# Attention's unit on TensorE in another order: 64-row products side by side, logits and places in a score bank

## Chip, cores and metric

One core of a Trainium2 chip. The metric is the device time of one execution in microseconds (us), as the median of several runs. Engines are called as the profile calls them: PE (TensorE's matmuls), PEld (its weight loads), DVE (VectorE), ACT (ScalarE), POOL (GpSimd), SP (SyncE).

## What is computed

Two residual layers over x of 32 sequences x 64 tokens x 512 channels. The first mixes each sequence with a chosen 64x64 matrix and applies a gated feed-forward block. The second is what the change touches: attention over a paged cache with a window of 256 keys, then a top-2 mixture over 8 experts.

```python
q, k, v = x @ Wq.T, x @ Wk.T, x @ Wv.T        # 8 query heads, 4 key heads of 64; rms norm and rotation of q and k
k_all, v_all = cache rows by block_tables, new k and v written in
scores = einsum('bghtd,bgsd->bghts', q, k_all) * SCALE      # masked to the last 256 positions
p = softmax(scores)
o = einsum('bghts,bgsd->bghtd', p, v_all) @ Wo.T
logits = clip(o @ gate_w.T, -50, 50)                        # 8 experts
top_w, top_idx = top_k(logits, 2)
rw = softmax(top_w)
out = x + o @ W.T + what the two chosen experts add, weighed by rw
```

## The kernel before

The program is written by hand for five engines. Each engine has a list of instructions that it runs in order, and semaphores tie the lists together: `wait_ge(s, n)` holds an engine's whole list until the counter s has reached n. There are three stages: layer 0 with the projections to q, k and v (to about 430 us), attention with routing (to about 770 us), and the experts. The change is in the second stage alone.

**Units.** Attention runs over `UNITS` = 64 units. Unit n takes the sequence q = n // 2 and one pair `gp` = n % 2 of the key heads. Four units (two sequences, 128 tokens) are a *pair* p = n // 4, and `at` = n % 4 is the unit's place in the pair. The loop over n on PE (L1017) is software-pipelined: its round n issues

- `score(n + 2)` (L924): six products of 320 columns, `q` by `kT`, over 64 rows (one head's 64 channels) each; the two heads lie in rows 0 to 63 and 64 to 127 and write banks 0 and 1;
- `turn_p(2n)` and `turn_p(2n + 1)` (L939): six transposes of the probabilities, over 128 rows;
- `turn_k(n + 3)` (L906): three transposes of the gathered keys. A sequence has 320 keys in three chunks of 128, 128 and 64 rows (`KCH`), so the third transpose, the *tail*, is over 64 rows;
- `values(n - 1)` (L947): the probabilities times the values, again in chunks of 128, 128 and 64 rows; each float32 product is two instructions in the trace, so that it shows six;
- at `at` = 0 `turn_q` (L917) for the next pair; at `at` = 2 `places(p - 2)` (L975), `logits(p - 1)` (L960) and `project_o(p - 1)` (L968), all over 128 rows.

**Where the keys and values come from.** POOL gathers each sequence's rows by indirect DMAs into a ring of `KVB` = 4 buffers `kv_t`: two from the cache (L541), one of new rows for the last chunk (L549), one that writes the routing list of an earlier pair from the tenth sequence on (L2084), and two that lay new rows over the cache's (L558), each of which waits until the cache's rows have landed. The gather of sequence q waits for `o_ps`, that is until the last product of `values` for sequence q - 4 has run; the transposes of its keys wait for `kv_gathered`:

```python
pool.wait_ge(o_ps, q - KVB + 1)                                  # L2091
pe.wait_ge(kv_gathered[q % KVB], (q // KVB + 1) * GATHERS)       # L910, in turn_k at gp == 0
```

So what `values` reads in the round with `at` = 2 of a pair (sequence 2p) is overwritten with sequence 2p + 4, whose keys `turn_k` takes in the round with `at` = 1 of the next pair.

**The other engines.** Per unit, ACT rounds the keys (`kT_hi`, L1197), takes exponentials (L1221) and copies the turned probabilities (`pT_copy`, L1224) and the result (`oT_copy`, L1233). DVE masks the scores (`masked`, L1780), scales the probabilities (`normalize`, L1789) and makes the low part of the keys (`kT_copy`, L1762), which the next `score` waits for. Its routing steps are `weigh`, `place_entry`, `read_logits`, `rank` and `choose` (L1804 to L1848). Logits, places and totals stand in bank 5, which also takes the turned keys; so `turn_k` at `at` = 3 waits for `lg_read`.

Of the kernel before, what the change touches and what calls it, by code (L numbers as in the profile page):

```python
# [83 lines left out]
def bass_adaln_ffn_kernel(nc, x, kv_lens, subjects, tables, cond_w, gate_t, up_t, down_t, gate_s, up_s, down_s,  # L84
# [20 lines left out]
    with ExitStack() as ctx:  # L105
# [508 lines left out]
        O_BANKS = (4, 7)  # L614

        def k_bank(n):

            return bk(2) if n == 1 else bk(5)
# [11 lines left out]
        with nc.Block() as block:  # L630
# [149 lines left out]
            def _(pe):  # L780
# [124 lines left out]

                def turn_k(n):  # L906

                    q, gp = n // 2, n % 2
                    if gp == 0:
                        pe.wait_ge(kv_gathered[q % KVB], (q // KVB + 1) * GATHERS)  # L910
                    if n >= 2:
                        pe.wait_ge(kT_ready, n)
                    for c, rows in enumerate(KCH):
                        mm = pe.transpose(k_bank(n)[:, c * P:c * P + rows], kv_t[q % KVB][0:rows, c, gp * P:(gp + 1) * P], ident[0:rows, 0:rows])  # L914
                    mm.then_inc(kT_ps, 1)
# [8 lines left out]
                def score(n):  # L924

                    p, b, gp = n // 4, n // 2 % 2, n % 2
                    if b == 0:
                        pe.wait_ge(qT_ready, p * 2 + gp + 1)
                    pe.wait_ge(kT_ready, n + 1)
                    if n >= 1:  # L930
                        pe.wait_ge(sm_ready, 2 * n)
                    for i, (q, k) in enumerate(((qT_hi, kT_hi), (qT_hi, kT_lo), (qT_lo, kT_hi))):
                        for g in range(2):
                            rows = slice(g * HD, (g + 1) * HD)
                            mm = pe.matmul(bk(g)[:, 0:KEYS], q[rows, gp, b, :, :].rearrange("p h t -> p (h t)"), k[rows, n % KRING, :],  # L935
                                           start=(i == 0), stop=(i == 2))
                    mm.then_inc(score_ps, 1)
# [22 lines left out]
                def logits(p):  # L960

                    pe.wait_ge(oT_ready, 2 * p + 2)
                    rows = oT if p < PAIRS - 1 else oT_last
                    for k in range(KT):
                        mm = pe.matmul(bk(5)[:, 0:E], rows[:, k, :, :].rearrange("p b t -> p (b t)"), wr[:, k, :], start=(k == 0), stop=(k == KT - 1))  # L965
                    mm.then_inc(lg_ps, 1)
# [8 lines left out]
                def places(p):  # L975

                    pe.wait_ge(sel_ready, p + 1)
                    pe.matmul(bk(5)[:, 2 * E:4 * E], tri[:, :], ab[:, :, :].rearrange("p a e -> p (a e)"), start=True, stop=False)
                    mm = pe.matmul(bk(5)[:, 2 * E:4 * E], ones_sq[:, :], counts[:, :, :].rearrange("p a e -> p (a e)"),
                                   start=False, stop=True)  # L980
                    if p == PAIRS - 1:
                        for n, part in enumerate((ab, counts)):
                            mm = pe.matmul(bk(5)[:, 4 * E:6 * E], ones_sq[:, :], part[:, :, :].rearrange("p a e -> p (a e)"),
                                           start=(n == 0), stop=(n == 1))
                    mm.then_inc(pos_ps, 1)
# [18 lines left out]
                fold(0)  # L1004
                fold(1)
                turn_k(0)
                turn_k(1)
                score(0)
# [4 lines left out]
                pe.wait_ge(counts_zero, 1)  # L1013
                pe.wait_ge(fold_ready, WR_DONE)
                turn_k(2)

                for n in range(UNITS):  # L1017
                    p, at = n // 4, n % 4
                    if n + 2 < UNITS:
                        score(n + 2)  # L1020
                    turn_p(2 * n)
                    turn_p(2 * n + 1)
                    if n + 3 < UNITS:
                        if at == 3 and p >= 1:
                            pe.wait_ge(lg_read, p)
                        turn_k(n + 3)
                    if n >= 1:
                        values(n - 1)
                    if at == 0 and p + 1 < PAIRS:
# [3 lines left out]
                    if at == 2 and p >= 1:  # L1033
                        pe.wait_ge(kT_ready, min(n + 4, UNITS))
                        if p >= 2:
                            places(p - 2)
                        logits(p - 1)
                        if p + 1 < PAIRS:
                            pe.wait_ge(qT_ready, 2 * p + 4)
                            project_o(p - 1)  # L1040

                final = PAIRS - 1
                values(UNITS - 1)
                places(final - 1)
                logits(final)
# [257 lines left out]
            def _(dve):  # L1303
# [500 lines left out]
                def read_logits(p):  # L1804
                    dve.wait_ge(lg_ps, p + 1)
                    dve.tensor_scalar(lg[:, :], bk(5)[:, 0:E], 50.0, -50.0, ALU.min, ALU.max).then_inc(lg_read, 1)

# [30 lines left out]

                def place_entry(p):
# [4 lines left out]
                    step(dve.tensor_tensor(chosen[:, :, :], bk(5)[:, 2 * E:4 * E].rearrange("p (a e) -> p a e", e=E), row_0[:, :, :], ALU.add),  # L1844
                         dve.tensor_tensor(counts[:, :, :], counts[:, :, :].bitcast(F32), ab[:, :, :].bitcast(F32), ALU.add))
                    step(dve.tensor_tensor(chosen[:, :, :], chosen[:, :, :], ab[:, :, :].bitcast(F32), ALU.mult))
                    step(dve.tensor_reduce(entry_row[:, p, :], chosen[:, :, :], AX, ALU.add))
# [39 lines left out]
                for n in range(UNITS):  # L1887
                    p, at = n // 4, n % 4
                    if at == 3 and p >= 1:
                        if p >= 2:  # L1890
                            place_entry(p - 2)
                        read_logits(p - 1)
                        rank(p - 1)
# [25 lines left out]
                dve.memset(seven[:, :], 0.0)  # L1919
                weigh(final - 1)  # L1920
                place_entry(final - 1)
                read_logits(final)
                rank(final)
                choose(final)
                weigh(final)
                place_entry(final)

# [7 lines left out]

                tstep(dve.tensor_scalar(total_i[:, :, :], bk(5)[:, 4 * E:6 * E].rearrange("p (a e) -> p a e", e=E), float(P - 1), None, ALU.add))
                tstep(dve.tensor_scalar(total_i[:, :, :], total_i[:, :, :], 7, None, ALU.arith_shift_right))
# [260 lines left out]
```

## Time and profile before

| | us |
|---|---|
| median of 3 runs | 949.13 |
| lowest, highest | 947.29, 950.86 |
| profiled execution, from its first to its last instruction | 947.2 |
| PE busy | 879.3 (93%) |
| PEld, DVE busy | 629.4, 658.1 |
| ACT, POOL busy | 385.0, 421.0 |

The page gives no time of the profiled execution other than its span; the lowest run is 0.1 us longer than it. A row of a timeline gives the start of a group of instructions in us from the span's start, how long the group lasted, its engine, line, operation and names, its shape as rows*columns, and in brackets how long the engine was idle before and what ended that. Ends of matmuls are modelled, so that on PE the distance from start to start tells more than the lengths.

### The profile page before, as it was taken

The page shows a single profiled execution, that of the slowest core. Times are in us where ns is not written, and L with a number is a line of the kernel's source. Part 1 is how long each engine was busy: PE and PEld are TensorE (multiplying, and loading weights), DVE is VectorE, ACT ScalarE, POOL GpSimd, SP SyncE. Part 2 cuts the span into 40 slices and gives each one's busy share as a digit, 9 for nine tenths or more (in the row PEclk, how much of TensorE's full clock was granted, in tenths as well). Part 3 has the DMA queues.
Part 4 walks back from the last instruction along what each step waited for, and adds up shares of the span by engine and source line. Part 5 has one row for each costly group of instructions (what it writes and reads, how often), then busy time and mean ns, then how long its engine had stood idle before and what let it go on. Part 6 is the DMA issues. An engine that isn't in the chain of part 4 may idle for free.

```text
span 947.2 us, 15001 instructions
## 1 busy us (share of the span) xinstructions
PE 879.3 (93%) x4053; PEld 629.4 (66%) x4053; DVE 658.1 (69%) x1897; ACT 385.0 (41%) x869; POOL 421.0 (44%) x478
## 2 busy tenths in 40 slices
PE   7799998999899999995899999999999986999994
PEld 6688746884688568743666666666666655888883
DVE  5754689966896699777778888888887772444441
ACT  3422233223222332285556666767766631111110
POOL 3312334444354400002454666656666424666873
PEclk9599999999999999997799999999999997999998
DMA  9645454013300410064332334434433105754772
GB/s 250 239 132 206 156 199 160 3 23 89 116 3 1 151 67 1 1 245 145 96 107 79 111 85 129 132 104 128 112 116 104 41 22 168 217 144 96 131 116 27
DMA packets 66360, 105.44 MB, mean 111 GB/s; under 512 B 29811, under 2 KB 31107, under 8 KB 66158
## 3 DMA queue, kind: packets, MB, share of 16 engines
q0 software_dynamic: 30368, 50.69, 21.2%
q1 hardware_dynamic: 34974, 52.14, 16.9%
q10 hardware_dynamic: 944, 1.74, 0.7%
q8 instruction: 32, 0.52, 0.3%
q14 instruction: 42, 0.34, 0.2%
HBM read 91.63 MB, written 37.49 MB: 136 GB/s over the span
## 4 chain that ended last, share of the span: by engine, by line
PE 74%; DVE 11%; DMA 5%; issue 5%; ACT 2%; SPq 1%; POOL 0%; DVEq 0%; POOLq 0%; ACTq 0%
PE bank L821 15%; PE bank L1071 13%; PE bank L955 11%; PE bank L832 8%; PE bank L972 6%; PE bank L944 5%; PE bank L935 4%; PE bank L854 3%; PE bank L914 3%; PE bank L1061 2%; DMA up_raw<-in_up_t 2%; DVE rot_b L1663 2%; DVE raw L1656 2%; PE bank L965 2%; PE bank L800 1%
## 5 line engine op out<-in xcount | busy, mean ns | idle before, releaser
L558 POOL DMA_INDIRECT kv_t<-kv_dram,own_new x64 | 64.8, 1013 | 143.1 <-DMA kv_dram<-kv_out 112.1
L854 PE MATMUL bank<-wqkv,x1T 128*128 128x512 f32 x256 | 112.1, 593 | 1.3 <-ACT x1T L1135 1.3
L955 PE MATMUL bank<-pT,kv_t 128*128 128x256 f32 (+1 forms) x384 | 112.1, 412 | 0.0
L541 POOL DMA_INDIRECT kv_t<-in_kv_cache,own_cache x64 | 66.0, 1031 | 81.5 <-PE bank L955 53.0
L1123 ACT ACTIVATE silu<-bank,gs 128x512 f32<-128x512 f32 x44 | 30.2, 690 | 156.8 <-PE bank L821 156.8
L1786 DVE CUSTOM_DVE_ANT_0 prob<-bank,mask 128x320 f32<-128x320 f32 x128 | 57.8, 489 | 50.6 <-PE bank L935 47.7
L854 PEld LDWEIGHTS bank<-wqkv,x1T 128*128 128x128 f32 x256 | 47.7, 190 | 57.4 <-issue 57.4
L955 PEld LDWEIGHTS bank<-pT,kv_t 128*128 128x128 f32 (+1 forms) x384 | 62.2, 187 | 28.9 <-issue 21.6
L821 PE MATMUL bank<-hT_hi,gate_w 128*128 128x512 f32 x176 | 72.1, 410 | 6.7 <-DVE hdn L1567 5.0
L1300 ACT ACTIVATE zT_hi<-bank 128x512 fp32r<-128x512 f32 x44 | 26.4, 599 | 122.7 <-PE bank L1061 122.7
L832 PE MATMUL bank<-down_w,hdn_hi 128*128 128x512 f32 x176 | 70.1, 398 | 4.0 <-DVE hdn_lo L1615 4.0
L1071 PE MATMUL bank<-experts_hi,zT_hi 128*128 x176 | 73.7, 419 | 0.0
L1221 ACT ACTIVATE prob<-prob,mx 128x320 f32<-128x320 f32 x128 | 70.9, 563 | 0.4
L821 PE MATMUL bank<-hT_lo,gate_w 128*128 128x512 f32 x176 | 70.4, 400 | 0.0
L1071 PE MATMUL bank<-experts_hi,zT_lo 128*128 x176 | 69.9, 397 | 0.0
L1071 PE MATMUL bank<-experts_lo,zT_hi 128*128 x176 | 69.5, 395 | 0.0
L832 PE MATMUL bank<-down_w,hdn_lo 128*128 128x512 f32 x176 | 69.3, 394 | 0.0
L821 PE MATMUL bank<-hT_hi,up_w 128*128 128x512 f32 x176 | 69.2, 393 | 0.0
L821 PE MATMUL bank<-hT_lo,up_w 128*128 128x512 f32 x176 | 69.1, 393 | 0.0
L1226 ACT ACTIVATE pT<-bank 128x384 f32<-128x384 f32 x128 | 56.0, 492 | 30.6 <-PE bank L944 30.3
L2045 POOL DMA_INDIRECT table_dram<-slot_val,slot_idx x32 | 56.8, 1775 | 25.3 <-POOL slot_val L2042 25.3
L1567 DVE SCALAR_TENSOR_TENSOR hdn<-bank,us,silu 128x512 f32<-128x512 f32 x44 | 33.0, 750 | 46.6 <-ACT silu L1123 45.2
(338 smaller groups left out, 2021.1 us busy)
## 6 DMA issues: line engine op xcount, KB each, us to landing
table_dram<-wexp POOLq DMA_DIRECT2D x16, 512.0 KB, 2.9
xr<-in_x SPq DMA_DIRECT2D x4, 1024.0 KB, 6.7
yx_dram<-x SPq DMA_DIRECT2D x16, 256.0 KB, 2.3
q_dram<-q_out SPq DMA_DIRECT2D x16, 256.0 KB, 2.1
kv_dram<-kv_out SPq DMA_DIRECT2D x16, 256.0 KB, 2.4
early_stage<-table_dram SPq DMA_DIRECT2D x8, 512.0 KB, 8.0
q_t<-q_dram SPq DMA_DIRECT2D x16, 256.0 KB, 2.7
stage<-table_dram SPq DMA_DIRECT2D x16, 256.0 KB, 3.1
```

Of the source, the lines that this page charges most:

```text
L541: pool.indirect_dma_start(kv_t[q % KVB][:, c, :], None, kv_cache, bass.IndirectOffsetOnAxis(own_cache[:, at:at + 1], 0), bounds_check=POOL ...
L558: pool.indirect_dma_start(kv_t[q % KVB][0:rows, c, :], None, kv_dram, bass.IndirectOffsetOnAxis(own_new[0:rows, at:at + 1], 0), bounds_che ...
L821: mm = pe.matmul(bk(2 * (i % 2) + half), w[:, k, i * P:(i + 1) * P], part[:, k, :].bitcast(form), start=(k == 0 and n == 0), stop=(k == KT ...
L832: mm = pe.matmul(bk(4 + j), part[:, i % 3, j * P:(j + 1) * P].bitcast(form), down_rows[:, i, :], start=(i == 0 and n == 0), stop=(i == IT ...
L854: mm = pe.matmul(bk(2 * (j % 2) + half), x1T[:, k, j * P:(j + 1) * P], wqkv[:, k, half * T:(half + 1) * T], start=(k == 0), stop=(k == KT ...
L955: mm = pe.matmul(bk(O_BANKS[q % 2])[:, gp * 2 * P:(gp + 1) * 2 * P], kv_t[q % KVB][0:rows, c, v:v + 2 * HD], pT[0:rows, n % 2, c, :, :].re ...
L972: mm = pe.matmul(bk(6), rows[:, k, :, :].rearrange("p b t -> p (b t)"), wo[:, k, :], start=(k == 0), stop=(k == KT - 1))
L1071: mm = pe.matmul(bk(4 + i % 2), y[:, i % 2, k, :], w[k][:, bass.ds(e, 1), :].rearrange("p a n -> p (a n)"), start=(k == 0 and n == 0), sto ...
L1221: act.activation(prob[s % PROBS][:, :], prob[s % PROBS][:, :], ACT.Exp, bias=mx[:, s % 8:s % 8 + 1], scale=-1.0, accum_out=rsum[:, s % 8:s ...
L1226: act.activation(pT[:, s // 2 % 2, :, s % 2, :], bk(2 + s % 2)[:, 0:NCH * P].rearrange("p (c t) -> p c t", c=NCH), ACT.Copy).then_inc(pT_r ...
L1786: dve.tensor_tensor_reduce(prob[s % PROBS][:, :], bk(s % 2)[:, 0:KEYS], mask[:, s // 4 % 2, :], MASKED, MASKED, ALU.add, ALU.min, mx[:, s ...
L2045: pool.indirect_dma_start(table_dram, bass.IndirectOffsetOnAxis(slot_idx[:, 0:1], 0), slot_val[:, :], None, compute_op=ALU.add).then_inc(e ...
```

## The change

In each round on PE the tail of `turn_k` becomes a function of its own, `turn_k_tail`, and stands right behind `score`; the two full transposes stay behind `turn_p`; and `values` moves to the end of the round, behind `turn_q` and behind places, logits and projection. The wait for `kv_gathered` goes with the tail. Logits, places and totals leave bank 5 for columns 320 and on of bank 0, one of the two score banks. Hence `places` and `logits` wait until DVE has read the score out of bank 0 (`sm_ready`), and the second score of each pair from the third on waits until DVE has read the logits (`lg_read`). On DVE `weigh`, the reading of the places (now `read_places`) and `read_logits` move to the round with `at` = 2, ahead of the pieces of the experts.

```diff
+        LG_AT = KEYS
+        PLACE_AT = LG_AT + 2 * E
+        TOTAL_AT = PLACE_AT + 2 * E
+        WHOLE = NCH - 1
...
-                def turn_k(n):
+                def turn_k_tail(n):
 
                     q, gp = n // 2, n % 2
                     if gp == 0:
                         pe.wait_ge(kv_gathered[q % KVB], (q // KVB + 1) * GATHERS)
                     if n >= 2:
                         pe.wait_ge(kT_ready, n)
-                    for c, rows in enumerate(KCH):
-                        mm = pe.transpose(k_bank(n)[:, c * P:c * P + rows], kv_t[q % KVB][0:rows, c, gp * P:(gp + 1) * P], ident[0:rows, 0:rows])
+                    c, rows = WHOLE, KCH[WHOLE]
+                    pe.transpose(k_bank(n)[:, c * P:c * P + rows], kv_t[q % KVB][0:rows, c, gp * P:(gp + 1) * P], ident[0:rows, 0:rows])
+
+                def turn_k(n):
+
+                    q, gp = n // 2, n % 2
+                    for c in range(WHOLE):
+                        mm = pe.transpose(k_bank(n)[:, c * P:(c + 1) * P], kv_t[q % KVB][:, c, gp * P:(gp + 1) * P], ident[:, :])
                     mm.then_inc(kT_ps, 1)
...
                     if n >= 1:
                         pe.wait_ge(sm_ready, 2 * n)
+                    if n % 4 == 1 and p >= 2:
+                        pe.wait_ge(lg_read, p - 1)
...
-                        mm = pe.matmul(bk(5)[:, 0:E], rows[:, k, :, :].rearrange("p b t -> p (b t)"), wr[:, k, :], start=(k == 0), stop=(k == KT - 1))
+                        mm = pe.matmul(bk(0)[:, LG_AT:LG_AT + E], rows[:, k, :, :].rearrange("p b t -> p (b t)"), wr[:, k, :], start=(k == 0), stop=(k == KT - 1))
...
                     if n + 2 < UNITS:
                         score(n + 2)
+                    if n + 3 < UNITS:
+                        turn_k_tail(n + 3)
                     turn_p(2 * n)
                     turn_p(2 * n + 1)
                     if n + 3 < UNITS:
-                        if at == 3 and p >= 1:
-                            pe.wait_ge(lg_read, p)
                         turn_k(n + 3)
-                    if n >= 1:
-                        values(n - 1)
                     if at == 0 and p + 1 < PAIRS:
                         if p >= 2:
                             pe.wait_ge(y_ready, p - 1)
                         turn_q(p + 1)
                     if at == 2 and p >= 1:
-                        pe.wait_ge(kT_ready, min(n + 4, UNITS))
+                        pe.wait_ge(sm_ready, 2 * min(n + 2, UNITS - 1) + 1)
                         if p >= 2:
                             places(p - 2)
                         logits(p - 1)
                         if p + 1 < PAIRS:
                             pe.wait_ge(qT_ready, 2 * p + 4)
                             project_o(p - 1)
+                    if n >= 1:
+                        values(n - 1)
...
                     if at == 3 and p >= 1:
                         if p >= 2:
                             place_entry(p - 2)
-                        read_logits(p - 1)
                         rank(p - 1)
...
+                    if at == 2 and p >= 1:
+                        if p >= 2:
+                            weigh(p - 2)
+                            read_places(p - 2)
+                        read_logits(p - 1)
                     if at == 2:
                         for m in (n - 2, n):
                             if low_item(m) < 0:
                                 early_low(AHEAD + m // 2)
                             elif low_item(m) < LATE:
                                 low_part(low_item(m))
-                        if p >= 2:
-                            weigh(p - 2)
```

The first place is PE in a round with `at` = 2 and the first instruction of the round behind it. Before:

```order
L935 MATMUL bank<-kT_hi,qT_hi 128x320 [waits sm_ready,kT_ready,qT_ready]
...
L944 MATMUL bank<-ident,prob_219 128x128 [waits pT_ready,prob_scaled]
...
L914 MATMUL bank<-ident,kv_t_214 128x128 [waits kT_ready]
...
L914 MATMUL bank<-ident,kv_t_214 128x64
L955 MATMUL bank<-pT,kv_t_185 128x256 [waits pT_ready]
...
L978 MATMUL bank<-ab,tri 128x16 [waits sel_ready,kT_ready]
...
L965 MATMUL bank<-wr,oT 128x8 [waits oT_ready]
...
L972 MATMUL bank<-wo,oT 128x512 [waits qT_ready]
...
L935 MATMUL bank<-kT_hi,qT_hi 128x320 [waits sm_ready,kT_ready,qT_ready]
```

The same round of the changed kernel (L948 is `score`, L919 the tail, L957 `turn_p`, L925 `turn_k`, L991 `places`, L978 `logits`, L985 `project_o`, L968 `values`):

```order
L948 MATMUL bank<-kT_hi,qT_hi 128x320 [waits sm_ready,kT_ready,qT_ready]
...
L919 MATMUL bank<-ident,kv_t_214 128x64 [waits kT_ready]
L957 MATMUL bank<-ident,prob_219 128x128 [waits pT_ready,prob_scaled]
...
L925 MATMUL bank<-ident,kv_t_214 128x128 x2
L991 MATMUL bank<-ab,tri 128x16 [waits sel_ready,sm_ready]
...
L978 MATMUL bank<-wr,oT 128x8 [waits oT_ready]
...
L985 MATMUL bank<-wo,oT 128x512 [waits qT_ready]
...
L968 MATMUL bank<-pT,kv_t_185 128x256 [waits pT_ready]
L968 MATMUL bank<-pT,kv_t_185 128x256 x2
L948 MATMUL bank<-kT_hi,qT_hi 128x320 [waits sm_ready,lg_read,kT_ready,qT_ready]
```

`values`, which stood ahead of places, logits and projection, now stands behind them, next to the score of the round that follows.

The second place is PE in the round with `at` = 1, up to `values`. Before:

```order
L935 MATMUL bank<-kT_hi,qT_hi 128x320 [waits sm_ready,kT_ready]
...
L944 MATMUL bank<-ident,prob_223 128x128 [waits pT_ready,prob_scaled]
...
L944 MATMUL bank<-ident,prob_192 128x128 [waits pT_ready,prob_scaled]
...
L914 MATMUL bank<-ident,kv_t_214 128x128 [waits kT_ready,kv_gathered2]
...
L955 MATMUL bank<-pT,kv_t_185 128x256 [waits oT_ready,pT_ready]
```

And now:

```order
L948 MATMUL bank<-kT_hi,qT_lo 128x320 x2
L919 MATMUL bank<-ident,kv_t_214 128x64 [waits kT_ready,kv_gathered2]
L957 MATMUL bank<-ident,prob_223 128x128 [waits pT_ready,prob_scaled]
...
L957 MATMUL bank<-ident,prob_192 128x128 [waits pT_ready,prob_scaled]
...
L925 MATMUL bank<-ident,kv_t_214 128x128 x2
L968 MATMUL bank<-pT,kv_t_185 128x256 [waits oT_ready,pT_ready]
```

The wait for the gathered rows (`kv_gathered2`) has moved ahead of the six transposes of `turn_p`.

## Rows read from the trace of the kernel before

**Rows 1.** The page, busy us of PE, its share of the span and its instructions.

```profile
PE 879.3 (93%) x4053; PEld 629.4 (66%) x4053; DVE 658.1 (69%) x1897; ACT 385.0 (41%) x869; POOL 421.0 (44%) x478
```

**Rows 2.** Timeline of PE over one pair of units, rounds at = 2, 3, 0, 1.

```profile
603.27 0.42 PE L935 MATMUL bank<-kT_hi,qT_hi 64*128 64x320 f32 x2 [0.38 <-issue]
...
605.13 1.76 PE L955 MATMUL bank<-pT,kv_t 128*128 128x256 f32 x6
606.82 0.28 PE L978 MATMUL bank<-ab,tri 128*128 128x16 f32 x1
...
611.57 0.41 PE L935 MATMUL bank<-kT_hi,qT_hi 64*128 64x320 f32 x2
...
612.91 0.58 PE L914 MATMUL bank<-ident,kv_t 128*128 128x128 f32 x3
613.43 1.76 PE L955 MATMUL bank<-pT,kv_t 128*128 128x256 f32 x6
614.82 0.51 PE L935 MATMUL bank<-kT_hi,qT_hi 64*128 64x320 f32 x2
...
615.56 0.88 PE L944 MATMUL bank<-ident,prob 128*128 128x128 f32 x6
...
616.78 1.76 PE L955 MATMUL bank<-pT,kv_t 128*128 128x256 f32 x6
618.47 0.66 PE L921 MATMUL bank<-ident,q_t 128*128 128x128 f32 x4
619.06 0.42 PE L935 MATMUL bank<-kT_hi,qT_hi 64*128 64x320 f32 x2
...
619.70 0.87 PE L944 MATMUL bank<-ident,prob 128*128 128x128 f32 x6
620.41 0.58 PE L914 MATMUL bank<-ident,kv_t 128*128 128x128 f32 x3
620.92 1.76 PE L955 MATMUL bank<-pT,kv_t 128*128 128x256 f32 x6
623.06 0.42 PE L935 MATMUL bank<-kT_hi,qT_hi 64*128 64x320 f32 x2 [0.38 <-issue]
```

**Rows 3.** Timeline of PEld, the weight load of one tail.

```profile
613.22 0.14 PEld L914 LDWEIGHTS bank<-ident,kv_t 64*128 64x128 f32 x1 [0.17 <-issue]
```

**Rows 4.** Timeline of DVE, the end of the round at = 1.

```profile
622.47 0.48 DVE L1764 TENSOR_TENSOR kT_lo<-bank,kT_hi 128x320 fp32r<-128x320 f32 x1
```

**Rows 5.** Timeline of POOL, the gather of one sequence.

```profile
607.76 1.02 POOL L541 DMA_INDIRECT kv_t<-in_kv_cache,own_cache  x1 [0.62 <-issue]
...
611.65 1.03 POOL L2084 DMA_INDIRECT list_dram<-entry,entry_at  x1 [0.30 <-DMA kv_t<-in_kv_cache,own_cache]
...
614.54 0.99 POOL L558 DMA_INDIRECT kv_t<-kv_dram,own_new  x1 [0.53 <-issue]
```

**Rows 6.** Line L558 from 600 to 640 us, its DMAs from issue to landing.

```profile
DMA to landing us min/median/max: 2.1/2.9/3.9
```

**Rows 7.** Waits of PE over the span: us in total, times, longest.

```profile
PE bank L914 <- DMA kv_t<-kv_dram,own_new: 5.2, 3, 3.1
```

**Rows 8.** Timelines of PE around three long idle times.

```profile
152.58 0.71 PE L821 MATMUL bank<-hT_hi,gate_w 128*128 128x512 f32 x1 [3.54 <-DVE hdn L1567]
...
255.31 0.79 PE L832 MATMUL bank<-down_w,hdn_hi 128*128 128x512 f32 x1 [2.25 <-DVE hdn_lo L1615]
...
474.11 0.64 PE L914 MATMUL bank<-ident,kv_t 128*128 128x128 f32 x3 [1.88 <-DMA kv_t<-kv_dram,own_new]
```

**Rows 9.** Busy time by stretch: PE, PEld, DVE, ACT, POOL, granted clock, DMA share, GB/s.

```profile
152.70:156.10 3.40, 3.40 (x9) 2.63 (x10) 2.95 (x7) 0.49 (x1) 1.16 (x3) 0.50 0.68 258
156.10:160.00 3.90, 3.90 (x19) 3.23 (x18) 3.63 (x12) 1.21 (x2) 2.91 (x2) 1.00 0.78 252
255.10:258.50 3.40, 3.19 (x8) 2.52 (x9) 3.13 (x9) 0.22 (x1) 0.00 (x0) 0.50 0.81 266
...
474.10:477.50 3.40, 3.39 (x21) 2.54 (x22) 1.62 (x5) 1.62 (x6) 2.07 (x3) 1.00 0.49 149
```

More of the change, by code:

```diff
@@ L977, in places @@
                     pe.wait_ge(sel_ready, p + 1)
-                    pe.matmul(bk(5)[:, 2 * E:4 * E], tri[:, :], ab[:, :, :].rearrange("p a e -> p (a e)"), start=True, stop=False)
-                    mm = pe.matmul(bk(5)[:, 2 * E:4 * E], ones_sq[:, :], counts[:, :, :].rearrange("p a e -> p (a e)"),
+                    pe.matmul(bk(0)[:, PLACE_AT:TOTAL_AT], tri[:, :], ab[:, :, :].rearrange("p a e -> p (a e)"), start=True, stop=False)
+                    mm = pe.matmul(bk(0)[:, PLACE_AT:TOTAL_AT], ones_sq[:, :], counts[:, :, :].rearrange("p a e -> p (a e)"),
                                    start=False, stop=True)
@@ L982, in places @@
                         for n, part in enumerate((ab, counts)):
-                            mm = pe.matmul(bk(5)[:, 4 * E:6 * E], ones_sq[:, :], part[:, :, :].rearrange("p a e -> p (a e)"),
+                            mm = pe.matmul(bk(0)[:, TOTAL_AT:TOTAL_AT + 2 * E], ones_sq[:, :], part[:, :, :].rearrange("p a e -> p (a e)"),
                                            start=(n == 0), stop=(n == 1))
@@ L1005, in _ @@
                 fold(1)
+                turn_k_tail(0)
                 turn_k(0)
+                turn_k_tail(1)
                 turn_k(1)
@@ L1014, in _ @@
                 pe.wait_ge(fold_ready, WR_DONE)
+                turn_k_tail(2)
                 turn_k(2)
@@ L1040, in _ @@
                             project_o(p - 1)
+                    if n >= 1:
+                        values(n - 1)
                 final = PAIRS - 1
                 values(UNITS - 1)
+                pe.wait_ge(lg_read, final)
                 places(final - 1)
@@ L1805, in read_logits @@
                     dve.wait_ge(lg_ps, p + 1)
-                    dve.tensor_scalar(lg[:, :], bk(5)[:, 0:E], 50.0, -50.0, ALU.min, ALU.max).then_inc(lg_read, 1)
+                    if p >= 1:
+                        dve.wait_ge(lg_exp, p)
+                    dve.tensor_scalar(lg[:, :], bk(0)[:, LG_AT:LG_AT + E], 50.0, -50.0, ALU.min, ALU.max).then_inc(lg_read, 1)
                 def rank(p):
@@ L1837, in weigh, with read_places @@
                     step(dve.tensor_reduce(entry[:, p, :, 1].bitcast(F32), chosen[:, :, :], AX, ALU.add))
-                def place_entry(p):
+                def read_places(p):
                     dve.wait_ge(pos_ps, p + 1)
@@ L1843, in place_entry @@
                         dve.wait_ge(lg_ps, p + 2)
-                    step(dve.tensor_tensor(chosen[:, :, :], bk(5)[:, 2 * E:4 * E].rearrange("p (a e) -> p a e", e=E), row_0[:, :, :], ALU.add),
+                    step(dve.tensor_tensor(chosen[:, :, :], bk(0)[:, PLACE_AT:TOTAL_AT].rearrange("p (a e) -> p a e", e=E), row_0[:, :, :], ALU.add),
                          dve.tensor_tensor(counts[:, :, :], counts[:, :, :].bitcast(F32), ab[:, :, :].bitcast(F32), ALU.add))
+                def place_entry(p):
                     step(dve.tensor_tensor(chosen[:, :, :], chosen[:, :, :], ab[:, :, :].bitcast(F32), ALU.mult))
@@ L1920, in _ @@
                 weigh(final - 1)
+                read_places(final - 1)
                 place_entry(final - 1)
@@ L1925, in _ @@
                 weigh(final)
+                read_places(final)
                 place_entry(final)
@@ L1934, in tstep @@
                     dve.wait_ge(tile_step, t.n)
-                tstep(dve.tensor_scalar(total_i[:, :, :], bk(5)[:, 4 * E:6 * E].rearrange("p (a e) -> p a e", e=E), float(P - 1), None, ALU.add))
+                tstep(dve.tensor_scalar(total_i[:, :, :], bk(0)[:, TOTAL_AT:TOTAL_AT + 2 * E].rearrange("p (a e) -> p a e", e=E), float(P - 1), None, ALU.add))
                 tstep(dve.tensor_scalar(total_i[:, :, :], total_i[:, :, :], 7, None, ALU.arith_shift_right))
```

## The prediction, made before the changed kernel was run

> **What bounds the kernel now.** I read the page first: PE is busy for 93% of the span [rows 1], so whatever shortens or holds PE moves the end. Then the timeline of PE over one pair [rows 2]: the score of the round at = 2 starts at 603.27 and the same one a pair later at 623.06, so a pair takes 19.79 us, in rounds of 8.30 (at = 2), 3.25 (at = 3), 4.24 (at = 0) and 4.00 (at = 1). PE is idle in it only once, 0.38 us ahead of the score at 623.06, and that score follows the end of `kT_lo` on DVE (622.47 + 0.48 = 622.95) by 0.11 us [rows 2, 4]. So three rounds are bound by PE's own products and the fourth by DVE. Last I read POOL, whose gathers bound nothing in a middle pair but come close: that is the step on which this forecast turns.
>
> **What a change of shape costs.** In the round at 611.57 the three transposes of `turn_k` take 612.91 to 613.43, 0.52 us. The six of `turn_p` take 0.71 (619.70 to 620.41), 0.12 each [rows 2]. So two full ones are 0.24 and the tail, 64 rows between products of 128 rows, is 0.28. Its weight load shows why: it starts only after 0.17 us of idle time [rows 3]. PE empties at the change of shape.
>
> **Term 1, the tail moved.** Behind the 64-row score it has no change ahead of it, and the one behind it was already paid by the score. Its price there is not in the trace: between 0.12 (a transpose among its like) and 0.28 (as now, and then nothing is gained). I take 0.13, near the lower end, because no drain is added: 0.15 saved per round, 0.60 per pair.
>
> **Term 2, `turn_q` moved ahead of `values`.** At = 0: values to `turn_q` 1.69 (616.78 to 618.47), its four transposes 0.59, the score behind it 0.64 (619.06 to 619.70), together 2.92. Without `turn_q`, values to score is 1.39 and that score 0.74 (613.43, 614.82, 615.56), together 2.13 [rows 2]. `turn_q` so adds 0.79, of which four transposes at 0.12 are 0.48. Saved: 0.31.
>
> **Term 3, places, logits and projection ahead of `values`.** Values to the first small product is 1.69 (605.13 to 606.82) against 1.39 to a score [rows 2]: 0.30, less 0.10 because a score right behind values takes 0.74 and not 0.64. Saved: 0.20. Terms 1 to 3 are 1.11 us per pair of PE's time.
>
> **Term 4, what moving `values` does to the gather.** At = 2, the end of `values` frees the buffer for the sequence that `turn_k` takes at = 1 of the next pair. Before, those products end at 605.13 + 1.76 = 606.89 [rows 2]. POOL's first issue is at 607.76, its last at 614.54, and that line's DMAs land 2.9 us after issue in the median [rows 5, 6]: all rows are there at 617.44, **10.55 us** after `values`. PE needs them at 620.41 [rows 2], 13.52 after `values`: 2.97 us to spare. With the fastest and slowest landing, 2.1 and 3.9 [rows 6], the gather takes 9.75 to 11.55.
>
> Now `values` stands behind the projection, at the end of the round, and the first transposed piece at = 1 is the tail, ahead of `turn_p`. Between them lie, without a wait: round at = 3, 3.25 - 0.15 = 3.10; round at = 0, 4.24 - 0.15 - 0.31 = 3.78; the score at = 1, 0.64; less 0.37, by which the last product of `values` ends after the next score starts (613.43 + 1.76 = 615.19 against 614.82 [rows 2]). That is 7.15 us, and the gather needs 10.55 + 0.11 to wake PE (as in rows 2 and 4). PE waits 3.5 us, once per pair, with `turn_p`, `turn_k` and `values` of that round queued behind the tail. That the same wait can hold PE is seen: three times, 5.2 us in all, the longest 3.1, before the ring is in step [rows 7].
>
> The pair is then a loop: gather 10.55, wake 0.11, from the tail to the next score 2.47 (tail 0.13 or so; 619.70 to 620.92 less 0.28 = 0.94; 1.39), and the round at = 2 to the end of its values, 8.30 - 0.15 - 0.20 + 0.37 = 8.32. Together **21.45 us against 19.79: +1.66 per pair**. The 1.11 saved and DVE's late `kT_lo` are inside this; DVE does its part of round at = 1 while PE waits.
>
> Thirteen pairs (1 to 13) have it: in pair 0 nothing stands ahead of `values` at = 2, and from pair 14 on no gather follows. In the first two POOL issues no list entry, which takes 1.03 + 0.30 [rows 5], so I put them at +0.33. Sum: 11 x 1.66 + 2 x 0.33 - 2 (the pairs outside the loop, which keep part of their saving) = **+17 us**.
>
> **Term 5, the clock.** A wait of 3.5 us shows as some 3.3 us of idle PE. Idle times of 3.54 and 2.25 us ended with the granted clock at 0.50, the level of 1.2 GHz instead of 2.4, for 3.4 us each; one of 1.88 did not [rows 8, 9]. In 3.4 us at half clock PE ran 9 and 8 products where 19 took 3.90 [rows 9]: 1.6 to 1.8 us lost, I take 1.7. It adds to the loop, because the tail, `values` and the projection lie behind the wait. Bounds: no fall, 0; a fall at each of 13 waits, +22. The wait lies between the two idle times that were followed by half clock, but those are only two; I take half the waits, **+11 us**. The Trainium skill, "TensorE: Matmul & The Clock Gate", section "HAM oscillation — how this bites in real kernels", speaks against this change more strongly: a kernel whose every round ends in a wait for a DMA loses the fast clock anew each round and pays half of the throttled time. By that rule the term would be the +22. The two long idle times here agree in kind, but neither was a wait for a DMA, and 1.88 us, which was one, kept the fast clock.
>
> The added waits cost nothing that I can see. The logits wait until DVE has read the score out of bank 0, which it must do for the same round anyway; the score behind waits for `lg_read`, and between places and the end of projection lie 4.75 us (606.82 to 611.57 [rows 2]) plus 1.39 of `values`. If that cover failed, rank and the two masks of the next round are queued behind the reading on DVE. ACT's copy of the result waits for the later `values` too, inside the stretch that the gather covers. POOL's second gather of the pair starts later, and its rows are wanted a whole pair later. SP's loads follow.
>
> Sum: 949.1 + 17 + 11 = **977 us**. It is made as a difference, so it applies to the profiled execution (span 947.2) as to the median, 1.9 us above it.
>
> **The rivals.**
> - *The clock holds.* The wait is there, no half clock behind it: 949 + 17 = 966. For it: 1.88 us of idle was borne [rows 8, 9].
> - *The clock falls behind each wait*: 949 + 17 + 22 = 988. For it: rows 8 and 9. The rule named under term 5 speaks for it.
> - *The other side: the gather comes in time.* Then the freed changes of shape set the time: 1.11 less 0.15 (round at = 1 stays with DVE's `kT_lo`) = 0.96 in 14 pairs, 949 - 13 = 936. It decides at 7.15 us from `values` to the last landing. Against it: POOL issues its last DMA 7.65 us after `values` ends (606.89 to 614.54), before any landing.
> - *No difference*: the gather shortens to about 8.9 us and the loop to 19.8. It would need a landing of some 1.3 us behind the last issue, below the 2.1 that was the least.
> - *The change of shape isn't freed*: a tail at 0.28 again gives up 0.60 per pair in rounds of which two lie in the gather's cover: +0.3 per pair, +4 us. Inside the range.
>
> **How the numbers follow.** A chance of 0.40 for half the falls (977), 0.25 for all (988), 0.23 for none (966), 0.07 for no difference, 0.05 for 936. The low end, 956, is the gather at 9.75 (+0.86 in 11 pairs, less 2) with no fall; at 11.55 (+2.66) and all falls it would be 1001, of which I cut the corner where both meet: 996. A measurement tells 0.5% from no change, 4.7 us; so faster 0.05, same 0.07, slower 0.88.
>
> **What would show it.** In the new profile, per pair: one wait of the tail (L919) for the gather's DMA, around 3.5 us, in round at = 1; rounds at = 3 and 0 no longer than before, at = 2 near 7.95; pairs of 21 to 23 us; half clock behind some waits. The weight load of the tail should have no idle time ahead of it. I am wrong if L919 doesn't wait, if PE waits for `lg_read` or `sm_ready` instead, or if the round at = 2 isn't shorter.

## The result, and the profile after

The changed kernel takes **998.25 us** (median of 4 runs, 994.54 to 1002.2) against 948.76 of the kernel before in the same session (4 runs, 947.29 to 950.86): a ratio of 1.0532, 95% interval 1.0506 to 1.0559. It is slower by 49.5 us. The direction was foretold; 977 was 21 us too low, and the range, 956 to 996, ended 2.25 us below the median. The profiled execution is the shortest of the four (span 992.9 us, time 994.54). Some executions are in a slower state of the chip; of all runs below only the longest of e4, 995.55 us, is counted as one.

The page of the changed kernel, to set beside [rows 1]: PE does the same 4053 products, is busy for 2.8 us less, and has 45.7 us more of span.

```profile
span 992.9 us, 15031 instructions
PE 876.5 (88%) x4053; PEld 644.8 (65%) x4053; DVE 658.4 (66%) x1897; ACT 388.2 (39%) x869; POOL 422.6 (43%) x478
...
PEclk7599999999999999985998898888899897999998
```

From the first score to the last, attention took 306.9 us before and takes 351.0: +44.1, so nearly all of it is there. The waits of PE from 500 to 800 us (us in total, times, longest) name above all one place, the tail of `turn_k` in the round at = 1:

```profile
PE bank L919 <- DMA kv_t<-kv_dram,own_new: 42.5, 13, 4.3
...
PE bank L948 <- DVE kT_lo L1781: 4.6, 12, 0.8
```

One pair on PE's timeline shows both losses. Each round begins with a score of L948, here at = 0 (543.87), at = 1 (547.51) and at = 2 (556.37):

```profile
543.87 0.41 PE L948 MATMUL bank<-kT_hi,qT_hi 64*128 64x320 f32 x2 [0.26 <-DVE kT_lo L1781]
...
547.51 0.41 PE L948 MATMUL bank<-kT_hi,qT_hi 64*128 64x320 f32 x2
...
552.46 0.37 PE L919 MATMUL bank<-ident,kv_t 64*128 64x64 f32 x1 [4.24 <-DMA kv_t<-kv_dram,own_new]
552.75 1.54 PE L957 MATMUL bank<-ident,prob 128*128 128x128 f32 x6
...
554.52 2.49 PE L968 MATMUL bank<-pT,kv_t 128*128 128x256 f32 x5
556.37 0.57 PE L948 MATMUL bank<-kT_hi,qT_hi 64*128 64x320 f32 x1
```

The tail begins 4.24 us late. Then PE's work is slow: the six transposes of `turn_p`, 0.71 before [rows 2], take 1.34 (552.75 to 554.09, where `turn_k` begins). The same place two hundred us later, behind a wait of 3.06, at full clock:

```profile
718.86 0.28 PE L919 MATMUL bank<-ident,kv_t 64*128 64x64 f32 x1 [3.06 <-DMA kv_t<-kv_dram,own_new]
719.07 0.87 PE L957 MATMUL bank<-ident,prob 128*128 128x128 f32 x6
```

The windows (busy us and instructions of PE, PEld, DVE, ACT, POOL, then granted clock, DMA share, GB/s) give the clock from 500 to 800 us, of the stretch around the first wait, of the one behind it, and of the one behind the second:

```profile
500.00:800.00 300.00, 252.68 (x1370) 179.37 (x1368) 206.36 (x837) 172.94 (x483) 154.34 (x153) 0.89 0.35 91
549.90:556.70 6.80, 4.24 (x15) 3.21 (x17) 1.54 (x6) 2.82 (x8) 4.97 (x6) 0.50 0.49 98
556.70:563.00 6.30, 6.30 (x35) 4.31 (x34) 4.83 (x20) 2.65 (x9) 0.50 (x1) 1.00 0.11 12
718.90:725.00 6.10, 6.10 (x42) 4.87 (x43) 3.02 (x11) 5.29 (x14) 4.58 (x6) 1.00 0.38 103
```

Before, the clock was 1.00 from 500 to 750 us, which leaves out the first 50 us of the stage and its last 7:

```profile
500.00:750.00 250.00, 244.99 (x1332) 159.47 (x1332) 201.56 (x816) 164.36 (x466) 151.11 (x150) 1.00 0.38 107
```

Eleven of the 13 waits (2.26 to 4.30 us each) came with half clock, which began in the wait or just behind it, 64.9 us in all. The release and POOL's side of the pair above: the last product of `values` let the buffer go at 540.6, POOL issued the gather from 541.47 to 548.03, and PE went on at 552.46, 11.9 us after the release.

```profile
540.22 0.38 PE L968 MATMUL bank<-pT,kv_t 64*128 64x256 f32 x1
...
541.47 1.00 POOL L541 DMA_INDIRECT kv_t<-in_kv_cache,own_cache  x1 [8.19 <-PE bank L968]
...
545.35 1.03 POOL L2110 DMA_INDIRECT list_dram<-entry,entry_at  x1 [0.30 <-issue]
...
548.03 1.01 POOL L558 DMA_INDIRECT kv_t<-kv_dram,own_new  x1 [0.30 <-issue]
```

Over the 13 pairs this took 9.7 to 12.0 us, 11.0 in the mean. Mean lengths in us of the rounds of the twelve middle pairs (n = 10 to 57), score to score, with the experiments. The stage of every kernel, the one before included, also has 12 to 18 us of half clock near its start, before 480 us; the last column counts from 480 us on:

| kernel | at = 2 | 3 | 0 | 1 | pair | stage | half clock from 480 us |
|---|---|---|---|---|---|---|---|
| before | 8.31 | 3.37 | 4.18 | 4.00 | 19.86 | 306.9 | 0 |
| changed | 7.87 | 4.07 | 3.68 | 7.65 | 23.27 | 351.0 | 64.9 |
| e1, values early at = 2 | 7.93 | 3.40 | 3.65 | 4.00 | 18.97 | 296.6 | 0 |
| e2, before + values late | 12.73 | 3.80 | 4.14 | 6.53 | 27.21 | 406.9 | 136.5 |
| e3, wait filled | 7.14 | 4.09 | 3.66 | 6.70 | 21.60 | 329.5 | 0 |
| e4, list entry behind | 7.78 | 4.17 | 3.72 | 6.47 | 22.13 | 336.9 | 44.4 |
| e5, e1 with the tail back | 8.30 | 3.40 | 3.68 | 4.16 | 19.54 | 303.3 | 0 |
| e6, values before `turn_q` too | 7.93 | 3.40 | 3.80 | 4.00 | 19.13 | 298.7 | 0 |
| e7, e1 with `kT_copy` first | 7.93 | 3.38 | 3.66 | 3.66 | 18.64 | 291.7 | 0 |
| e8, wait half filled | 7.36 | 4.10 | 3.69 | 6.64 | 21.79 | 332.4 | 10.2 |
| e9, before + tail | 8.21 | 3.33 | 3.80 | 4.00 | 19.34 | 301.2 | 3.4 |
| e10, before + bank | 8.29 | 3.43 | 4.16 | 4.00 | 19.88 | 306.5 | 0 |

### The profile page after: what moved, and what is told of

Same layout as the page of the kernel before. It is cut to its first block, busy times and chain, and to the rows that moved or that the text cites. A ratio compares the mean times of both kernels' runs of the same rounds, so it can differ in the third digit from the quotient of the medians.

```text
span 992.9 us, 15031 instructions
## 1 busy us (share of the span) xinstructions
PE 876.5 (88%) x4053; PEld 644.8 (65%) x4053; DVE 658.4 (66%) x1897; ACT 388.2 (39%) x869; POOL 422.6 (43%) x478
## 4 chain that ended last, share of the span: by engine, by line
PE 63%; DVE 11%; DMA 11%; issue 8%; ACT 2%; POOL 2%; SPq 1%; POOLq 0%; DVEq 0%; ACTq 0%
PE bank L826 14%; PE bank L1088 12%; PE bank L837 8%; PE bank L968 7%; PE bank L985 6%; DMA kv_t<-kv_dram,own_new 5%; PE bank L957 4%; PE bank L859 3%; DMA kv_t<-in_kv_cache,own_cache 3%; PE bank L948 2%; DMA up_raw<-in_up_t 2%; PE bank L1078 2%; DVE raw L1673 2%; DVE rot_b L1680 1%; PE bank L978 1%
## 5 line engine op out<-in xcount | busy, mean ns | idle before, releaser
L558 POOL DMA_INDIRECT kv_t<-kv_dram,own_new x64 | 66.8, 1044 | 140.6 <-DMA kv_dram<-kv_out 112.1
L968 PE MATMUL bank<-pT,kv_t 128*128 128x256 f32 (+1 forms) x384 | 121.2, 441 | 0.0
L968 PEld LDWEIGHTS bank<-pT,kv_t 128*128 128x128 f32 (+1 forms) x384 | 72.4, 214 | 37.0 <-issue 32.1
```

Of the source, the lines that this page charges most:

```text
L558: pool.indirect_dma_start(kv_t[q % KVB][0:rows, c, :], None, kv_dram, bass.IndirectOffsetOnAxis(own_new[0:rows, at:at + 1], 0), bounds_che ...
L968: mm = pe.matmul(bk(O_BANKS[q % 2])[:, gp * 2 * P:(gp + 1) * 2 * P], kv_t[q % KVB][0:rows, c, v:v + 2 * HD], pT[0:rows, n % 2, c, :, :].re ...
```

## The experiments

**e1: `values` back ahead of the routing products in the round at = 2**, the rest as changed.

```diff
                     if at == 2 and p >= 1:
+                        values(n - 1)
                         pe.wait_ge(sm_ready, 2 * min(n + 2, UNITS - 1) + 1)
...
-                    if n >= 1:
+                    if n >= 1 and not (at == 2 and p >= 1):
                         values(n - 1)
```

> The changed kernel, but in the round at = 2 the values products stand ahead of places, logits and projection again; everything else of the change stays. Theory (the late values make the gather late, and PE waits for it): the 42.5 us of idle PE ahead of the tail between 500 and 800 us goes to under 5 us, no half clock is left there, a pair takes 18.5 to 19.2 us, and the time is 932 to 940 us. Rival (the waits that the score bank brings, lg_read and sm_ready, or the new changes of shape cost the time): the time stays above 980 us.

Measured: 940.28 us (937.61 to 943.72, 5 runs) against 946.78, ratio 0.9935 (0.9905 to 0.9965). Waits of PE from 500 to 750 us:

```profile
PE bank L948 <- issue: 7.4, 11, 0.7
...
PE bank L919 <- DMA kv_t<-kv_dram,own_new: 1.3, 3, 0.6
```

The time is 0.3 us above the range that I had expected. The wait for the gather goes from 42.5 us to 1.3 and half clock from 64.9 us to none. This one place of `values` is the whole loss; what else the change does is a gain.

**e2: the kernel before with only that move.**

```diff
                         if p + 1 < PAIRS:
                             pe.wait_ge(qT_ready, 2 * p + 4)
                             project_o(p - 1)
+                        values(n - 1)
```

(and the old call skipped at = 2.)

> The kernel before, with one edit: in the round at = 2 the values products stand behind the projection. No tail moved, no bank changed. Theory (late values alone do it): turn_k at = 1 waits for the gather some 3 us in 13 pairs, half clock follows, 985 to 1010 us. Rival (the score bank or the tail's place is needed for the loss): 945 to 960 us.

Measured: 1049.74 us (1045.41 to 1055.38), ratio 1.1103 (1.1045 to 1.116); even worse than expected. Waits from 500 to 850 us:

```profile
PE bank L914 <- DMA kv_t<-kv_dram,own_new: 31.3, 13, 4.3
...
PE bank L978 <- DVE kT_lo L1765: 15.9, 13, 1.5
```

The move alone makes the wait for the gather. It also makes a second one: in the kernel before, places waits until `kT_lo` has been read out of bank 5, and `values` was the cover of that. With logits and places in bank 0 that wait is gone. So the new bank, which by itself gives nothing (e10), spares the late `values` this second wait. Half clock is twice that of the changed kernel, 136.5 us against 64.9, although the waits are shorter in the mean: 2.4 us for the gather (31.3 / 13) and 1.2 for `kT_lo` (15.9 / 13). So the loss in e2 is more than the wait that I had forecast.

**e3 and e8: the wait filled with products.** 24 (e8: 14) transposes of the identity into free columns, ahead of the tail of the round at = 1, from the third pair on.

```diff
+                    if at == 1 and p >= 2:
+                        for _ in range(FILL):
+                            pe.transpose(bk(5)[:, 3 * P:4 * P], ident[:, :], ident[:, :])
                     if n + 3 < UNITS:
                         turn_k_tail(n + 3)
```

> The changed kernel with 24 idle transposes of the identity (2.6 us of PE work that nobody reads, into spare columns of bank 5) just ahead of the tail's wait at = 1, so that PE is busy in most of the wait. Theory with the clock (some 65 us of half clock lie between 500 and 800 us, and they cost 20 to 28 us): the granted clock stays at 1.00 there, pairs fall from 23 to 24 us to 21 to 22, and the time is 968 to 978 us although the work has grown. Rival (the clock costs little, the whole loss is the wait): 995 to 1005 us.

> e3_filled_wait with 14 transposes instead of 24 (1.5 us of PE work instead of 2.6), so that some 1.5 to 2.5 us of the wait stay idle. If that keeps the fast clock, 966 to 973 us, since the filler no longer lengthens short waits; if the clock falls behind the rest of the wait as in the changed kernel, 980 to 992.

Measured: e3 972.47 us (968.82 to 973.77), ratio 1.0259 (1.0223 to 1.0294); e8 971.17 (969.15 to 975.22), 1.0259 (1.0228 to 1.0291). Windows of e3, then of e8, and e8's wait:

```profile
500.00:780.00 280.00, 267.39 (x1695) 197.49 (x1693) 207.42 (x843) 171.88 (x484) 155.24 (x154) 1.00 0.38 98
```

```profile
500.00:780.00 280.00, 256.43 (x1550) 185.48 (x1548) 206.71 (x837) 170.88 (x481) 153.02 (x152) 0.98 0.38 96
```

```profile
PE bank L920 <- DMA kv_t<-kv_dram,own_new: 18.2, 13, 2.7
```

The gather is as late as ever: in the middle pairs the tail starts 11.1 us after the release in the mean in both kernels (11.12 in the changed one, 11.16 in e3). What shrinks lies behind it, from the tail to the next score (3.60 to 2.61) and from there to the end of `values` (8.56 to 7.83). So work that nobody needs makes the kernel some 24 us shorter, and with it the half clock is gone. That parts the loss in two: the changed kernel less e3 is the clock, 21.5 us by the stages (351.0 - 329.5) and 23.8 by the medians, each against the kernel before of its own session (49.5 - 25.7); e3 less before is the wait, 22.6 by the stages and 25.7 by the medians. e8 leaves 18.2 us of idle time in the 13 places, none over 2.7, and has 10.2 us of half clock. Less idle time came with less half clock, but no single length decides: in e8 the longest wait, 2.71 us, kept the fast clock, and one of 1.75 (ended at 591.32) had half clock behind it.

**e4: the list entry behind the gather.** POOL issues the routing list's DMA after the new rows' instead of ahead of them.

```diff
+                        gather_new(pool, q)
                         if p >= LISTED_BEHIND:
...
-                        gather_new(pool, q)
```

> The changed kernel with POOL's list entry issued behind the two last gather DMAs instead of ahead of them. Theory (POOL's own issue time of 1.33 us counts in the gather): rows land up to 1.3 us sooner, idle PE ahead of the tail falls from 42.5 to about 30 us, 975 to 990 us. Rival (the landing of the cache's rows, not POOL's issues, sets the end of the gather): within 3 us of the changed kernel, 995 to 1001.

Measured: 978.71, 978.82, 988.28 and 995.55 us, median 983.55, ratio 1.0388 (1.0319 to 1.0457); without the longest the median is 978.82, a ratio of 1.034. The granted clock over the whole execution was 0.929, 0.936, 0.917 and 0.917. The profile is of the run of 978.82. The wait of PE, and the clock from 500 to 780 us:

```profile
PE bank L919 <- DMA kv_t<-kv_dram,own_new: 32.5, 14, 3.6
```

```profile
500.00:780.00 280.00, 242.21 (x1332) 171.58 (x1330) 203.73 (x818) 167.56 (x468) 154.17 (x152) 0.92 0.37 96
```

A gather shorter by one DMA takes 10 us from the wait and 20.5 from the half clock: the two shrink together.

**e5, e6, e7: what is left of the gain, on top of e1.** e5 puts the tail back behind the full transposes (the wait for the gather stands ahead of those again), e6 puts `values` ahead of `turn_q` too, and e7 lets DVE make `kT_lo` ahead of the two scalings of the round at = 1.

```diff
 # e5
                     if n + 3 < UNITS:
-                        turn_k_tail(n + 3)
...
                         turn_k(n + 3)
+                        turn_k_tail(n + 3)
 # e6, every round
+                    if n >= 1:
+                        values(n - 1)
                     if at == 0 and p + 1 < PAIRS:
 # e7, DVE
+                    if at == 1 and n + 3 < UNITS:
+                        kT_copy(n + 3)
...
-                    if n + 3 < UNITS:
+                    if at != 1 and n + 3 < UNITS:
                         kT_copy(n + 3)
```

> e1_values_early with the tail put back behind the two full transposes of turn_k, its wait for the gather with it; the rest stays. Prediction's term 1 says 0.15 us per round lost, 0.60 per pair, 9 us: 949 us. Rival from the traces of before and e1 (rounds at = 3 and 1 kept 3.25 and 4.00 us, set by kT_lo and not by PE's products): only the rounds at = 2 and 0 lose, 0.3 per pair, 4 to 5 us, 943 to 946.

> e1_values_early with values ahead of turn_q as well, so that values stands where it stood in every round and only the tail and the score bank remain of the change. Term 2 says the round at = 0 loses 0.31 us, 5 us in 15 pairs: 944 to 946 us. Rival (kT_lo bounds that round too, or the gather gains from earlier values): within 2 us of e1, 939 to 942.

> e1_values_early with DVE making kT_lo ahead of the two normalize steps in the round at = 1 (where the next score waits 0.7 us for it). Theory (that round is DVE's order, not its work): 4.00 falls to about 3.3 us, some 9 us over 15 pairs, 930 to 934 us, the fastest so far. Rival (the probabilities come later instead and turn_p waits for them, or the gather now binds): 938 to 942 us.

Measured, against 947.26 before: e5 945.16 us (942.07 to 948.62, 12 runs), ratio 0.9974 (0.9956 to 0.9992); e6 939.4 (934.71 to 941.59), 0.9913 (0.9888 to 0.9938); e7 933.62 (931.56 to 937.97), 0.986 (0.9834 to 0.9886). The round at = 2 of e1, then of e5:

```profile
600.56 0.87 PE L957 MATMUL bank<-ident,prob 128*128 128x128 f32 x6
601.27 0.38 PE L925 MATMUL bank<-ident,kv_t 128*128 128x128 f32 x2
601.49 1.66 PE L968 MATMUL bank<-pT,kv_t 128*128 128x256 f32 x6
603.07 0.28 PE L991 MATMUL bank<-ab,tri 128*128 128x16 f32 x1
```

```profile
604.41 0.38 PE L919 MATMUL bank<-ident,kv_t 128*128 128x128 f32 x2
604.72 0.27 PE L925 MATMUL bank<-ident,kv_t 64*128 64x64 f32 x1
604.92 1.76 PE L967 MATMUL bank<-pT,kv_t 128*128 128x256 f32 x6
606.61 0.28 PE L990 MATMUL bank<-ab,tri 128*128 128x16 f32 x1
```

From `turn_k` to `values` 0.22 us against 0.51, from `values` to places 1.58 against 1.69. That is 0.29 + 0.11; less some 0.03 for the tail behind the score (score to `turn_p` is 0.67 here, 599.89 to 600.56, and 0.64 without a tail [rows 2]) it makes the difference of the two rounds, 8.30 - 7.93 = 0.37. So e5 is the rival of its expectation, 943 to 946, and not the 949 of term 1; e6 is its rival too, within a microsecond of e1: `values` ahead of `turn_q` or behind it makes no difference that can be told. In the rounds at = 3 and 0 of e1 little or nothing of it is left. PEld's waits in e1 from 500 to 745 us, and the first product of one score behind a round at = 3, say why:

```profile
PEld bank L948 <- DVE kT_lo L1782: 11.0, 26, 0.8
```

```profile
611.52 0.41 PE L948 MATMUL bank<-kT_hi,qT_hi 64*128 64x320 f32 x2 [0.43 <-DVE kT_lo L1782]
```

Twice in each of 13 pairs the first load of the next score waits for `kT_lo`. The shorter rounds had been within a few tenths of DVE's end. e7 takes DVE's part forward: at = 1 falls from 4.00 to 3.66 (I had expected about 3.3) and the stage by another 4.9 us. It is the fastest version found, and then the gather begins to hold PE, a little (waits from 500 to 740 us):

```profile
PE bank L919 <- DMA kv_t<-kv_dram,own_new: 4.9, 6, 1.4
```

**e9 and e10: one part of the change on the kernel before.** e9 moves the tail alone, e10 the bank alone (with its waits and DVE's reads).

```diff
 # e9
                     if n + 3 < UNITS:
+                        turn_k_tail(n + 3)
+                    turn_p(2 * n)
+                    turn_p(2 * n + 1)
 # e10
-                        mm = pe.matmul(bk(5)[:, 0:E], rows[:, k, :, :].rearrange("p b t -> p (b t)"), wr[:, k, :], start=(k == 0), stop=(k == KT - 1))
+                        mm = pe.matmul(bk(0)[:, LG_AT:LG_AT + E], rows[:, k, :, :].rearrange("p b t -> p (b t)"), wr[:, k, :], start=(k == 0), stop=(k == KT - 1))
```

> The kernel before with the tail alone moved (behind score, with its wait for the gather, and the wait for lg_read ahead of it); values, logits and places stay where they were. Theory (the tail is what gains, 0.37 us in rounds where PE's products bind, seen as 8.30 against 7.93 at = 2 between e5 and e1): 940 to 944 us. Rival (the score bank is needed for that): 945 to 949.

> The kernel before with logits, places and totals in the score bank alone, and DVE's routing steps where the change has them; the tail and values stay where they were. Theory (the bank frees a wait of places for kT_lo that other work covered): within 3 us of the kernel before, 944 to 949. Rival (the bank and DVE's earlier reading shorten the rounds at = 3 and 0): 938 to 943.

Measured, against 948.24: e9 940.43 us (935.36 to 942.37), ratio 0.9902 (0.9872 to 0.9932); e10 949.15 (945.76 to 951.73, 12 runs), 1.0013 (0.9993 to 1.0032). By the medians the tail alone gives what e1 gives. In the one profile of each it gives less, 5.7 us of the stage against 10.3; some 2 us of that are one round at = 2 of 10.13 us, with half clock in it, where the eleven others took 8.03 or 8.04. Logits and places in bank 0 give and cost nothing by themselves: the median is 0.15 us above the range expected and the interval takes in 1.

## Why the prediction was right, and where it was wrong

**What held.** The direction and the mechanism did: one wait per pair, of the tail for the gather's last DMA, in 13 pairs, from the later release of the buffer. So did the price of a wait at full clock, a pair of 21.45 us against 21.60 in e3, where the clock held. That agreement is partly luck, since misses cancel. The means of e3's middle pairs are 11.16 from the release to the tail's start where I had 10.55 + 0.11, then 2.61 to the next score where I had 2.47, and 7.83 for the round at = 2 to the end of its `values` where I had 8.32. The longer gather is seen in the changed kernel too: the DMAs of L558 land after 3.3 us in the median and 5.2 at most, against 2.9 and 3.9 [rows 6]; why, no run here shows. PE shows no wait for `sm_ready` or `lg_read`, as said, and the tail's weight load has no idle time ahead of it but these 13 waits. The round at = 2 came out at 7.87, near the 7.95 forecast, but that is luck: half clock is in it, and in e3 it took 7.14.

**The step that failed is term 5: "I take half the waits, +11 us".** Measured: 11 of 13, worth 21.5 us by the stages. The price of one fall, 1.7 us, was near (21.5 / 11 = 1.95), although eight of the eleven stretches are 6.8 us long, where I had read 3.4 from [rows 9]: 15.5 of the 64.9 us lie within the waits, where PE has nothing to run. I set two falls [rows 8, 9] against one idle time of 1.88 us and took the middle, though that one was shorter than every wait forecast. Length alone settles no single case: of the waits here those of 2.39 and 3.06 us kept the fast clock and one of 2.26 did not, and the wait of 1.88 us that was followed by full clock in the kernel before [rows 8, 9] is there again in the changed one, just as long, with half clock behind it (468.10 to 471.40):

```profile
467.35 0.28 PE L919 MATMUL bank<-ident,kv_t 64*128 64x64 f32 x1 [1.88 <-DMA kv_t<-kv_dram,own_new]
```

```profile
468.10:471.40 3.30, 3.30 (x14) 2.35 (x14) 0.66 (x2) 2.44 (x7) 1.82 (x3) 0.50 0.38 120
```

But of these 13 waits, 3.3 us in the mean (42.5 / 13), eleven came with half clock, and half of them was the forecast. The rule weighed under term 5, from the Trainium skill's "TensorE: Matmul & The Clock Gate", section "HAM oscillation — how this bites in real kernels", is that such a loop loses the fast clock anew in each round and pays half of the throttled time. The trace agrees in the main on the first, 11 waits of 13, and not on the second: half of 64.9 us is 32.4, and 21.5 was measured. The rival of all falls (988) had the right mechanism and a chance of 0.25; it was still 10 us low, half of it by term 4. The other half is the difference between the medians, 49.5 us, and the stages of one execution each, 44.1.

**Term 4's sum was low too**: +17, measured +22.6 (e3 less before, by the stages). Per pair it was right: from release to release, in e3 less before, the eleven pairs with a list entry grew by 1.75 in the mean, against +1.66. The deductions were not right. The two pairs ahead of them, put at +0.33 each, grew by 1.03 and 1.61; and what lies ahead of the first of these pairs and behind the last, for which I took 2 us off, added 0.7.

**The range** failed by the corner that was cut: the long gather with all falls, "1001", was written down and left out as if the two were independent. e4 shows that they go together: a gather shorter by one DMA came with less wait and with less half clock. The profiled execution lies inside the range, the median just above it.

**Terms 1 to 3.** Term 1 was too small where PE decides and too large where it does not. At = 2 a moved tail saves 0.37 (e1 against e5), not 0.15. Its old place gave 0.29, as read (0.28); its new one costs some 0.03, where I took 0.13; and the 0.11 from `values` to places was not priced at all. In the kernel before, with the old bank, it saves 0.27 in most pairs (8.30 to 8.03, e9). At = 3 it saves nothing, since the sentence "three rounds are bound by PE's own products" was true by a margin of tenths only; behind it DVE's `kT_lo` binds. At = 0 the two savings don't add: the tail alone gives 0.38 (e9), `turn_q` ahead of `values` alone 0.50 (e5), both 0.53 (e1), and kT_lo ends that round too. The nearest run to the rival with the gather in time, 936, is e1, which lacks term 3: 940. Term 3 is read from e3, whose round at = 2 begins at 596.71 and runs at full clock:

```profile
602.86 1.44 PE L969 MATMUL bank<-pT,kv_t 128*128 128x256 f32 x5
603.82 0.41 PE L949 MATMUL bank<-kT_hi,qT_hi 64*128 64x320 f32 x1
...
604.13 0.38 PE L969 MATMUL bank<-pT,kv_t 64*128 64x256 f32 x1
...
604.78 0.21 PE L920 MATMUL bank<-ident,kv_t 64*128 64x64 f32 x1
```

The last products of `values`, over 64 rows, run among those of the score, also over 64. The round at = 2 gains 7.93 - 7.14 = 0.79 against e1; the score behind it, which takes 0.96 to its tail (603.82 to 604.78) instead of 0.54 (607.82 to 608.36 in e1), gives 0.42 back to the round at = 3. Left are 0.37, against the 0.20 of term 3.

**A miss without a price.** The round at = 3 was to shrink to 3.10 and grew to 4.07. Of this 0.42 is the slower score just seen. The rest is in the queues of DVE and ACT:

```profile
540.63 0.77 ACT L1259 ACTIVATE oT<-bank 64x256 f32<-64x256 f32 x2 [4.31 <-PE bank L968]
...
541.51 0.49 DVE L1803 CUSTOM_DVE_ANT_0 prob<-bank,mask 128x320 f32<-128x320 f32 x1 [0.22 <-DVE gtr L1836]
...
542.66 0.46 ACT L1214 ACTIVATE kT_hi<-bank 128x320 fp32r<-128x320 f32 x1
...
543.33 0.48 DVE L1781 TENSOR_TENSOR kT_lo<-bank,kT_hi 128x320 fp32r<-128x320 f32 x1
```

The score at 543.87 waits for `kT_lo`. DVE starts its first mask right behind a step of `rank`, 1.60 us after the score of this round (539.91), where it was 0.89 in most rounds of e1, and from there to `kT_lo` it has no idle time. ACT alone would have held the round nearly as long: `oT_copy` now waits for the late `values` (4.31 us idle), the keys' `kT_hi` is behind it and ends 3.21 us into the round instead of 2.65. In the last of the twelve rounds DVE was ready sooner and waited for `kT_hi`; that round took 3.78 us, the others 3.96 and more. All of it lies in the stretch that the gather covers, so the sum doesn't change; the prediction named ACT's copy as covered and did not see that it delays the next score.

## What to carry to other kernels

Before a product is moved, ask which buffer its end frees and who is queued on that buffer: here some 3.3 us of waiting a pair cost more than all changes of shape together, and with that product left in place the rest of the change is a gain. A wait of some 3 us, once per pair, was paid about twice here, 22.6 us as the wait and 21.5 as half clock; products that nobody needs, put into the wait, told the two apart. Terms that grow from the same cause belong in the same corner of the range.

## What was not expected of the hardware

- Of the 11 stretches of half clock the eight that began while PE still waited (as at 549.90, with the tail at 552.46) lasted 6.8 us, and the three that began behind the wait's end (as at 505.5, with the tail at 504.77) lasted 3.4.
- Fourteen transposes in a wait of some 3.3 us were enough to keep most of the fast clock (0.98 against 0.89 granted).
- Half clock also came without a long wait: in e9 it was 0.50 from 586.3 to 589.5 us, in a round whose longest idle times of PE were 0.73 us ahead of its score and 0.44 ahead of places. What brought it is open.
- A 64-row transpose behind 64-row products cost 0.03 to 0.06 us (score to `turn_p` 0.67 to 0.70 in e1, against 0.64 [rows 2]), less than a 128-row one among its like (0.12), where between 128-row products it was 0.28.
